# Eight tiled mask products instead of two whole ones, and rope tables renewed one at a time

## The reference, cut to what matters

```python
q = l2norm(q) * qs;  k = l2norm(k) * ksc            # qs, ksc: one vector of 64 per layer
q = q * cos * scale + rotate_half(q) * sin * scale  # k with 1/scale
# windows of 32 queries, each against its own 32 keys and the 32 before them
mask = (it < jb) | (it > jb + w) | (jb == -1)
sim  = einsum('bhwie,bhwje->bhwij', bq, bk2) * 8.0
sim  = where(mask, -max, sim);  attn = softmax(sim);  out = attn @ bv2
```

## Time and profile before

| what | value |
|---|---|
| median of 3 runs | 3816.27 us (3815.24 to 3817.18) |
| profiled execution, its own time | 3817.41 us |
| its span, first to last instruction | 3815.5 us |
| mean granted TensorE clock | 0.981 of 2.4 GHz |
| busy: PE / DVE / ACT / POOL | 93% / 82% / 69% / 63% |
| L1158, mask products | 384, 114.2 us busy |
| L1164, score products | 24576, 287.0 us busy |
| L878, rope tables | 24, 12.3 us busy |

### The profile page before, as it was taken

How to read it: one execution, slowest core, us unless ns; L and a number is a source line. 1 busy time by engine, 2 the same in 40 slices (tenths; PEclk the granted TensorE clock), 3 DMA queues, 4 the chain that set the end, 5 groups by cost and what they waited for, 6 DMA issues and landing times.

```text
span 3815.5 us, 146379 instructions
## 1 busy us (share of the span) xinstructions
PE 3549.1 (93%) x60112; PEld 2231.2 (58%) x60128; DVE 3112.5 (82%) x4377; ACT 2650.5 (69%) x4972; POOL 2420.8 (63%) x2197
## 2 busy tenths in 40 slices
PE   5667676899999999999999999999999999999997
PEld 2222222466666666666666666666666666666664
DVE  4899998888888888888878888878888788888884
ACT  3545454677777777777777777777777777777775
POOL 0356555776666666666666666666666666666661
PEclk9889899999999999999999999999999999999999
DMA  3000000010111111111111111111111111111101
GB/s 78 0 0 0 0 0 0 26 37 28 33 35 48 37 33 32 32 48 37 37 33 32 43 43 35 30 32 32 48 41 34 32 32 48 37 37 29 33 28 38
DMA packets 64418, 120.05 MB, mean 31 GB/s; under 512 B 18196, under 2 KB 35986, under 8 KB 63634
## 3 DMA queue, kind: packets, MB, share of 16 engines
q1 hardware_dynamic: 63762, 110.70, 10.0%
HBM read 20.50 MB, written 2.10 MB: 6 GB/s over the span
## 4 chain that ended last, share of the span: by engine, by line
PE 79%; issue 2%; DVE 2%; ACT 1%; POOL 0%; DMA 0%; ACTq 0%; POOLq 0%; DVEq 0%; SPq 0%
PE qk L1130 17%; PE trb L1002 10%; PE ob L1188 10%; PE vob L1196 8%; PE vob L1136 8%; PE sc L1164 7%; PE sc L1215 6%; PE ob L1002 4%; PE sc L1222 3%; PE sc L1158 2%; PE vob L1238 1%; PE vob L1250 1%; DVE arena L889 0%; DVE ssq L895 0%; DVE arena L890 0%
## 5 line engine op out<-in xcount | busy, mean ns | idle before, releaser
L507 POOL TENSOR_TENSOR arena<-arena,rnorm 128x512 f32<-128x512 f32 x768 | 785.2, 1044 | 930.0 <-ACT rnorm L626 929.5
L500 POOL TENSOR_TENSOR arena<-arena 128x512 f32<-128x512 f32 x768 | 962.8, 1275 | 35.9 <-DVE arena L890 35.9
L633 ACT ACTIVATE arena<-trb 128x512 f32<-128x512 f32 x768 | 462.6, 602 | 441.6 <-PE trb L1002 441.6
L1130 PE MATMUL qk<-wqkv,xs 128*128 128x512 f32 x1536 | 729.4, 597 | 16.3 <-issue 9.2
L889 DVE TENSOR_TENSOR arena<-qk,tab_q 128x512 f32<-128x512 f32 x384 | 263.3, 686 | 455.0 <-ACT arena L619 447.6
L483 POOL TENSOR_TENSOR arena<-arena 128x512 f32<-128x512 f32 x256 | 300.0, 1182 | 346.4 <-DVE arena L859 333.8
L1002 PE MATMUL trb<-ident,arena 128*128 128x128 f32 x3072 | 482.3, 280 | 9.8 <-ACT arena L633 7.3
L1130 PEld LDWEIGHTS qk<-wqkv,xs 128*128 128x128 f32 x1536 | 292.7, 191 | 309.1 <-issue 291.7
L895 DVE TENSOR_REDUCE ssq<-arena 128x16 f32<-128x1024 f32 x384 | 463.7, 1207 | 0.0
L619 ACT ACTIVATE arena<-qk 128x512 f32<-128x512 f32 x768 | 426.8, 588 | 45.0 <-PE qk L1130 28.1
L1002 PEld LDWEIGHTS trb<-ident,arena 128*128 128x128 f32 x3072 | 346.7, 141 | 140.1 <-issue 88.3
(11 more groups left out here) (139 smaller groups left out, 5879.6 us busy)
## 6 DMA issues: line engine op xcount, KB each, us to landing
arena<-arena SPq DMA_DIRECT2D x192, 384.0 KB, 3.2
arena<-arena SPq DMA_DIRECT2D x192, 64.0 KB, 3.0
wqkv<-in_L_ffn_Wqkv SPq DMA_DIRECT2D x18, 512.0 KB, 4.6
wo<-in_L_ffn_Wo SPq DMA_DIRECT2D x6, 512.0 KB, 4.0
arena<-in_L_attn_x SPq DMA_DIRECT2D x8, 256.0 KB, 2.9
out<-arena SPq DMA_DIRECT2D x8, 256.0 KB, 2.2
w<-in_L_ffn_W SPq DMA_DIRECT2D x6, 341.0 KB, 2.9
arena<-in_sel SPq DMA_DIRECT2D x1, 1024.0 KB, 5.0
```

What stands on the lines that cost most here:

```text
L500: nc.gpsimd.tensor_tensor(ts[c * 2 + j][:, heads], tu[:, 0, heads], tu[:, 1, heads], ALU.add).then_inc(summed[0], 1)
L507: nc.gpsimd.tensor_tensor(part, part, rnorm[j][:, 8 * h:8 * h + 8].unsqueeze(2).to_broadcast([P, 8, HEAD]), ALU.mult) \
L633: A((qT, kT)[j][u][:, 4 * h:4 * h + 4, at_col:at_col + P], TRB.rearrange("p (a t) -> p a t", a=4), ACT.Copy) \
L1130: MM(QK[:, 512 * h:512 * h + 512], lhsT=xs[u][:, c * P:(c + 1) * P], rhs=wqkv[:, col:col + 512], start=True, stop=True) \
```

## The change

Three edits:

1. The mask goes into the score banks by eight products instead of two. Each has a 64x32 piece of the identity as its stationary operand and 64 partitions of the mask as the moving one, 512 columns as before. They use the same eight tiles of the array, in the same order, as the score products behind them. For g = 0 the identity's piece picks the mask rows 0 to 31 of its half, for the others the rows 32 to 63. The constant `mask` is changed so that both halves of its partitions hold the first window's pattern in rows 0 to 31 and the general one in rows 32 to 63.
2. A semaphore increment `s_open`, on which nobody waits, stands in front of the mask products.
3. The rope tables are renewed one piece at a time. Each of the last four slots of a layer is followed, one slot later and behind `square_sums`, by the renewal of the piece that this slot's unit was the last to use. The first layer's pieces are made before the stack begins. In each of a layer's first four slots, DVE waits for the one piece that it needs.

```diff
+        s_open = sem("s_open")
@@ vector engine
-            def layer_tables(l, layer):
-
-                for c in range(CHUNKS):
-                    for tab, base, sc in ((tab_q, base_q, scale_q), (tab_k, base_k, scale_k)):
-                        V.tensor_tensor(tab[:, c], base[:, c], sc[:, ds(layer, 1), :].to_broadcast([P, 2, HEAD]), ALU.mult) \
-                            .then_inc(tabs_done[0], 1)
+            def layer_table(layer, c, j):
+
+                tab, base, sc = (tab_q, tab_k)[j], (base_q, base_k)[j], (scale_q, scale_k)[j]
+                V.tensor_tensor(tab[:, c], base[:, c], sc[:, ds(layer, 1), :].to_broadcast([P, 2, HEAD]), ALU.mult).then_inc(tabs_done[0], 1)
@@ layer_slot of the vector engine
-                if unit and k % LAYER == 0:
-                    layer = l + k // LAYER
-                    if k:
-                        item(dve, roped, unit[0] * 2 + -1)
-                    layer_tables(l, layer)
-                    item(dve, tabs_done, layer * (2 * CHUNKS) + (2 * CHUNKS - 1))
+                if unit and k % LAYER < UNITS:
+                    dve.wait_ge(tabs_done[0], (l + k // LAYER) * UNITS + k % LAYER + 1)
                 if unit:
                     rope(*unit)
...
                 if unit:
                     square_sums(*unit)
+                ahead = unit_at(l, k, 1)
+                if ahead and not isinstance(l, int) and LAYER - UNITS <= (k - 1) % LAYER:
+                    item(dve, roped, ahead[0] * 2 + 1)
+                    layer_table(l + 1, ahead[3], ahead[4])
...
             dve.wait_ge(cleared[0], 2)
+            for c in range(CHUNKS):
+                for j in range(2):
+                    layer_table(0, c, j)
             item(dve, ln_out, 2 * GROUPS - 1)
@@ scores, tensor engine
-                for h in range(2):
-                    MM(SC[:, 512 * h:512 * h + 512], lhsT=ident16[:], rhs=mask[:, :].unsqueeze(1).to_broadcast([P, STEP_PAIRS, 2 * SPAN]),
-                       start=True, stop=True)
+                pe.sem_inc(s_open[0], 1)
+                for g in range(4):
+                    for h in range(2):
+                        d, pick = slice(64 * h, 64 * h + 64), 64 * h + (WINDOW if g else 0)
+                        MM(SC[32 * g:32 * g + 32, 512 * h:512 * h + 512], lhsT=ident16[d, pick:pick + WINDOW],
+                           rhs=mask[d, :].unsqueeze(1).to_broadcast([64, STEP_PAIRS, 2 * SPAN]), start=True, stop=True, skip_group_check=True)
@@ constants
-    inside &= (i >= WINDOW) | (k >= SPAN) | (k % SPAN >= WINDOW)
+    inside &= (i % SPAN >= WINDOW) | (k >= SPAN) | (k % SPAN >= WINDOW)
```

## The result

The changed kernel takes 3793.24 us (median of 6 runs, 3790.27 to 3797.34); the kernel before, on the same chip, 3816.72 us (6 runs, 3815.24 to 3819.90). The ratio is 0.9938, interval 0.9925 to 0.9951: 23.5 us saved. The forecast was 3778.5, so 14.7 us of the expected gain did not come. The profiled executions are 3817.41 before and 3797.34 after (span 3795.5, the slowest of its six), 20.1 apart.

A forecast was written before the change was run, and what follows sets the result against it. TensorE's own list was taken to set the time from 730 to 3742 us. 189 steps x 0.20 = 37.8 us off 3817.41 gave 3779.6, or 3778.5 as median; own range 3773 to 3787, 8 in 10 3758 to 3799.

The forecast's parts named there:

- What bounds the kernel: From 730 to 3742 us, 79% of the span, TensorE's own list of work sets the time.
- The mask products: Eight tiled mask products run side by side in one stream of 0.215 us instead of 0.43; 0.20 a step taken.
- Rivals 2 and 3: Mask on tiles: array halves take turns, nothing saved, 3816 to 3828, 6%; or eight run one after another, 4060, 6%.
- the 0.065 a step: Saving if each of six more mask products cost 60 cycles, 0.15 us together; result about 3804.
- The pause: Switch between whole array and tiles, about 0.09 us, moves from behind the mask to in front; counted as nothing.
- The queue of pairs: Ready load-and-product pairs at the score block: eight mask pairs leave 24 score pairs instead of 32; new ones come 0.010 us apart.
- The first reading: Queue places free only when a product ends: flow back at 0.46, last score start 1.49 us after the first mask product.
- rival 1: Pair arrivals hide behind the mask: 0.35 a step saved, about 3756; 15% with values between.
- The third reading: Six more mask pairs paid in full at 0.010 us each: 0.155 saved a step.
- `s_open`, the tables: Increment before the mask costs 0, at most 0.1 a step; rope tables 0, bounds -1 to +5 us over five layers.
- What is late next: Engines following TensorE get 0.2 us less per step; tightest room found 0.60 and 0.38 us, so no other wait takes over.
- Rival 4: A wait from ACT, DVE or the loop's four gaps eats TensorE's saving: 15 us saved, 3801; 11% with savings of 0.05 to 0.15 a step.

The follow-up runs named there:

- e1: Kernel before with only the eight mask products changed, rope tables renewed as before: 3797.16 us, ratio 0.9940 to the kernel before.
- e2: Kernel before with only the rope tables changed, mask still by two products: 3823.71 us, ratio 1.0006 to the kernel before.
- e5: Changed kernel with the eight mask products written twice in a row: 3851.25 us, a single run.
- e6: Changed kernel with 16 mask products of 256 columns instead of eight of 512, all with start=True: 3818.34 us, ratio 0.9992 to the kernel before.
- e3: Changed kernel with 128 idle semaphore increments at the start of TensorE's list: 3812.18 us, ratio 0.9977 to the kernel before.
- e10: Changed kernel run once more, unaltered: 3792.98 us, ratio 0.9930 to the kernel before.
- e4: Kernel before with 128 idle semaphore increments at the start of TensorE's list: 3842.23 us, ratio 1.0061 to the kernel before.
- e12: Changed kernel with 16 mask products of 256 columns, only the first eight with start=True: 3819.17 us, a single run.
- e8: Changed kernel with 192 idle semaphore increments in TensorE's list in front of the scan: 3816.23 us, ratio 0.9988 to the kernel before.
- e7: Changed kernel with 64 idle semaphore increments in TensorE's list in front of the scan: 3802.73 us, ratio 0.9960 to the kernel before.

## Why the prediction was right, and where it was off

- **What bounds the kernel.** Right: only what left TensorE's own list moved the time (e1 against e2), and what took some of it back is TensorE's own too, its stalls and its clock.
- **The mask products.** Right and slightly undersized: 0.230 a step, where I took 0.20. Eight starts in 23 ns, first score 227 ns after the first mask (forecast 0.215), and e5 prices eight products at 0.215. Rivals 2 and 3 fall with the same rows: the h = 0 and h = 1 products start 3 ns apart. So does the 0.065 a step that followed from the Trainium skill, "TensorEngine Tiling (Array Packing)", section Instruction Overhead: the trace does not agree with 60 cycles for each product on different tiles, since the starts are 3 ns apart and a step saved 0.230.
- **The pause** moved from behind the mask to in front of it: 429 became 523 ns, forecast 0.43 and 0.52.
- **The queue of pairs.** The first reading fits best. The ready scores shrank from 32 to 24, as forecast: by the medians of the starts they come in groups of eight, 0.056 apart, up to the 24th at 0.403 after the first mask product, and more slowly behind it. The flow came back 0.41 to 0.43 after that product (forecast 0.46, rival 1: 0.33), some 0.03 behind the end of its 0.386, and the last score started 1.469 after it (forecast 1.49, rival 1: 1.36). The third reading, a charge of 0.06 for six pairs, did not come: that would have been 0.155 a step. The 3 ns for eight pairs in e6 are no clean price, since its shorter products would let the flow return sooner by the first reading. Without the charge it is 0.215 a step, and the earlier return of the flow would account for the rest; that part is argued, not shown.
- **`s_open`, the tables.** At nothing, as said (e1, e2, and the distances above hold no room for the increment). `s_open` was not taken out by itself.
- **"What is late next ... So nothing takes over."** This is the step that failed. I looked for a late engine and found room everywhere, rightly: the stalls go by the place in the list and not by an engine's work (e3). What took over is TensorE's own supply of instructions, which the sum had at nothing. With the clock behind the edges (some 4.7 us by the estimate above) it took 17.3 of the 43.9 us, at the same five steps in two executions (e10), and e3 moves it by moving the list. The forecast had the four "issue" gaps of the earlier trace rows in view and added nothing for them to grow; e4 shows them at 14.1 instead of 9.2 after a mere shift. Rival 4 ("a wait that moves in ... or the loop's four gaps", 3801) had the right sign and reason in its last words, and the result lies between it and the forecast, outside the forecast's own range (3773 to 3787) and inside the range for 8 in 10.
- **Luck.** That so much of the gain came is in part a matter of position. The same products 128 instructions further on take 8 us more from the first mask product to the end (e3), and the kernel before, so shifted, 17 (e4). The forecast had no term for that, in either direction.
- **The tail** cost the first profiled execution another 6.4 us at a mean clock of 0.82. That fits with this execution (3797.34) being the slowest of its six.

With the measured terms the sum is 43.9 - 17.3 - 2.3 to 6.4 for the tail, or 20 to 24 us; measured, 23.5.

The Trainium skill, "Runtime: NRT & Kernel Launch", section Instruction fetch mechanics, says that instructions come in 16 KiB blocks of 256, that crossing a border is mostly hidden because the engine issues more slowly than the blocks come, and that a taken branch can break this. The block size and the stalls at the loop's edges agree with the traces here (16 KB packets; waits of 2.1 to 3.7 us at the edges). "Hidden" holds for most blocks, but not where 272 short instructions run in 1.6 us. Read beside the earlier trace rows, where 256 of them run in 1.28 us, this section of the Trainium skill could have led to a term of the right sign, though not to its size.

## What to carry to other kernels

Where TensorE's list sets the time and its neighbours are tiled, a whole-array product can be traded for tiled products side by side at the price of one stream; a change of mode only moves. Price the instructions too: where more than a block of them runs faster than a block arrives, part of the gain is lost again to stalls, and any edit ahead of them shifts them by luck, some 15 us here. Look at the granted clock right behind a wait as well, since a wait can cost more than its own length. A stall that returns at the same place in each iteration, whose named releaser ended well before it did, is to be tested by shifting the list, not by speeding up the engine named.

## What the runs showed of the hardware

- Products on different tiles start 3 ns apart for eight bf16 products of 512 columns, and the next round follows 0.215 to 0.227 us later (e5): the eight write into two banks at once without taking turns.
- A later start=True product into the second half of a bank makes later products overwrite the first half instead of adding to it: the mask of that half is lost in e6 and takes full effect in e12, and the two differ in that flag alone. The Trainium skill, "PSUM — Partial Sum Buffer", section The four PSUM rules, says so: such a product clears the written marks of the whole bank in its quadrants. The pair of runs agrees with it, for 256 columns on each side; the contents of the bank itself are in no trace.
- Semaphore increments in a row start 0.15 us apart in TensorE's list, though the record of each is 51 ns long. Here are the 192 of e8 in front of the scan and the 128 of e3 at the start of the list (first and last start in us):

```profile
L1104 PEldq EVENT_SEMAPHORE  x192: 51/51/51, 102.0 to 131.5; - x192
...
L1001 PEldq EVENT_SEMAPHORE  x128: 51/51/51, 2.5 to 21.9; - x128
```

  What they cost is what sticks out of a wait that stands there anyway. At the start of the list the first transfer lets PE begin only at 17.5 us, so the 19.4 us of e3 move its first product by 5.0, to 22.5. In front of the scan PE waits 7.3 to 8.8 us for ACT in the changed kernel: 64 increments (e7) leave it at 8.8, and 192 make it 26.4.
- One of the loop's edges (2428 us of the first profile) was 3.7 us long, and the product blocks behind it ran at half clock: the step's scores took 2.05 instead of 1.46 us. In e10 the clock fell behind three edges, after waits of 2.1 to 2.5 us, and stayed up behind the one of 2.7 us. So the length of the wait alone does not decide it.
